# Gathered rows of the expert stages: transposed by DMA transfers instead of TensorE and ScalarE

## The reference

```python
x = x + xattn(layernorm(x), ctx)      # differential attention, 16 heads, 77 context rows per batch
# mixture of experts on h = layernorm(x), 2048 tokens, 8 experts of width 1024, two experts per token
probs = softmax(h @ gate_w.T); w, idx = top_k(probs, 2); w = w / sum(w)
for e in range(8):
    g, u = split(h @ gate_up[e].T)    # 256 -> 1024 and 1024
    acc += combine[:, e] * (silu(g) * u @ down[e].T)
x = x + acc
```

## Time and profile before

| | |
|---|---|
| median of 3 runs | 634.52 us (633.24 to 636.4) |
| profiled execution, its time | 635.76 us |
| profiled execution, span from first to last instruction | 634.0 us |
| granted TensorE clock, mean over the span | 0.905 |

### The profile page before, as it was taken

One profiled execution on the slowest core, in us unless ns is written; L12 is line 12 of the kernel. 1 busy time (PEld: TensorE's weight loads), 2 busy tenths in 40 slices (PEclk: granted clock), 3 DMA queues, 4 the chain that ended last, 5 costly groups with the idle time before them and its releaser, 6 DMA issues.

```text
span 634.0 us, 12250 instructions
## 1 busy us (share of the span) xinstructions
PE 508.0 (80%) x3882; PEld 376.9 (59%) x3897; DVE 419.5 (66%) x883; ACT 347.7 (55%) x653; POOL 253.1 (40%) x237
## 2 busy tenths in 40 slices
PE   3673798899899878601388999998999999999980
PEld 2452555666666644501266777776887777877750
DVE  6445448888888765589268888785655656646551
ACT  1210568678677577200178878775656565655530
POOL 4000634344333334100322665445555456544334
PEclk9985689898898799655799999999999999999996
DMA  4368676766756541140134776645323233332323
GB/s 160 123 167 186 183 201 173 213 161 189 210 149 179 151 151 43 42 141 0 43 89 149 173 166 158 156 105 125 60 54 56 46 66 52 59 51 44 34 24 43
DMA packets 57563, 72.55 MB, mean 114 GB/s; under 512 B 18649, under 2 KB 42841, under 8 KB 57369
## 3 DMA queue, kind: packets, MB, share of 16 engines
q1 hardware_dynamic: 45984, 56.03, 31.1%
q0 software_dynamic: 11520, 15.74, 14.9%
HBM read 49.08 MB, written 22.41 MB: 113 GB/s over the span
## 4 chain that ended last, share of the span: by engine, by line
PE 54%; DVE 17%; ACT 8%; issue 5%; DMA 4%; POOL 1%; SPq 0%; ACTq 0%; POOLq 0%; DVEq 0%
PE bank L1257 19%; PE bank L1273 10%; PE bank L1124 4%; PE bank L1110 4%; PE bank L1133 3%; PE bank L1147 3%; PE bank L1078 3%; DMA out<-FB,slot_tok 2%; DVE FB L1021 2%; DVE WE L877 2%; DVE FB L1017 2%; PE bank L1092 2%; PE bank L1228 2%; PE bank L1140 2%; PE bank L1284 1%
## 5 line engine op out<-in xcount | busy, mean ns | idle before, releaser
L1257 PE MATMUL bank<-FB,WE 128*128 128x0 bf16 x1440 | 188.5, 281 | 1.3 <-ACT FB L723 1.2
L1257 PEld LDWEIGHTS bank<-FB,WE 128*128 x1440 | 137.0, 98 | 30.7 <-issue 2.0
L1017 DVE TENSOR_TENSOR FB<-FB,bank 128x512 f32<-128x512 f32 x120 | 82.5, 687 | 105.2 <-ACT FB L730 100.4
L591 POOL DMA_INDIRECT out<-FB,slot_tok x60 | 95.7, 1595 | 103.6 <-DVE FB L1029 95.1
L730 ACT ACTIVATE FB<-bank 128x512 f32<-128x512 f32 x120 | 71.7, 598 | 102.3 <-PE bank L1257 91.3
L1273 PE MATMUL bank<-FB,WE 128*128 128x0 bf16 x720 | 104.1, 280 | 13.3 <-DVE FB L1021 10.3
L582 POOL DMA_INDIRECT FB<-x_parts,slot_tok x60 | 63.9, 1066 | 100.0 <-PE bank L1228 48.2
L1273 PEld LDWEIGHTS bank<-FB,WE 128*128 x720 | 63.8, 97 | 42.1 <-issue 27.2
L1021 DVE TENSOR_TENSOR FB<-FB 128x512 bf16<-128x512 f32 x120 | 82.4, 687 | 0.0
L525 POOL TENSOR_TENSOR WE<-FB,WE 128x1024 bf16<-128x1024 f32 x26 | 55.5, 2138 | 58.5 <-ACT WE L622 58.5
L736 ACT ACTIVATE FB<-FB 128x512 bf16<-128x512 f32 x120 | 74.9, 624 | 0.2 <-DVE FB L1017 0.2
(11 more groups left out here) (173 smaller groups left out, 660.2 us busy)
## 6 DMA issues: line engine op xcount, KB each, us to landing
FB<-w SPq DMA_DIRECT2D x26, 512.0 KB, 5.8
WE<-w SPq DMA_DIRECT2D x44, 256.0 KB
WE<-q_parts SPq DMA_DIRECT2D x32, 200.0 KB
WE<-x SPq DMA_DIRECT2D x16, 256.0 KB, 4.9
q_parts<-FB SPq DMA_DIRECT2D x32, 128.0 KB
x_parts<-WE SPq DMA_DIRECT2D x20, 128.0 KB, 4.2
out<-WE SPq DMA_DIRECT2D x20, 128.0 KB, 4.5
q_parts<-WE SPq DMA_DIRECT2D x16, 128.0 KB
```

Source lines behind the costliest of these rows:

```text
L591: pool.indirect_dma_start(out=out, out_offset=bass.IndirectOffsetOnAxis(ap=slot_tok[:, c:c + 1].bitcast(U32), axis=0), in_=y_sb[c % 2], in ...
L1017: nc.vector.tensor_tensor(hid[k % 2], hid[k % 2], up_bank[k % 2][1][:, :], ALU.mult).then_inc(h_ready, 1)
L1257: ins = nc.tensor.matmul(to, wf[:, bass.ds(at + o, P)], xgT[s % 2][:, 2 * part + kc, :].shape_from_register(long[s % 2]), start=(z == 0), ...
```

## The change

A tile is turned by four DMA transfers with `transpose=True`, from `xg[c % 2]` straight to the four blocks of `xgT[s % 2]`, issued on SP's queue. Each moves 128 rows by 128 bf16 values, 32 KB. The TensorE transposes and the ScalarE copies are gone, and with them the PSUM bank between them. Two semaphores `xg_turned`, one for each parity of the tile number, take the place of `xgt_mm` and `xgT_ready`. The late loads are now issued in one loop with the turning: four ahead, then stage 0's four tiles, then for each k the tile k % 8 of stage k // 8 + 1 (for k % 8 < 4), and behind it late load k + 4.

```diff
+            def turn_tile(s, i):
+
+                c = SUB * s + i
+                sp.wait_ge(xg_in[c % 2], 16 * (c // 2 + 1))
+                if s >= 2:
+                    sp.wait_ge(g_mm, FC * (s - 1))
+                for k in range(4):
+                    sp.dma_start(xgT[s % 2][:, k, i * P:(i + 1) * P], xg[c % 2][:, k * P:(k + 1) * P], transpose=True).then_inc(xg_turned[c % 2], 16)
+
+            def park_in():
+                sp.wait_ge(split_out, 64)
+                sp.wait_ge(late_lo, len(LATE))
+                sp.dma_start(WE[:, E - 1, 2 * W1N:EW], wd).then_inc(parked_in, 16)
+
-            for j in range(len(LATE)):
+            for j in range(LSTG):
                 load_late(j)
-            sp.wait_ge(split_out, 64)
-            sp.wait_ge(late_lo, len(LATE))
-            sp.dma_start(WE[:, E - 1, 2 * W1N:EW], wd).then_inc(parked_in, 16)
+            sp.wait_ge(idx_ready, 1)
+            for i in range(SUB):
+                turn_tile(0, i)
+            for k in range(FC * (NS - 1)):
+                if k % FC < SUB:
+                    turn_tile(k // FC + 1, k % FC)
+                if LSTG + k < len(LATE):
+                    load_late(LSTG + k)
+                if k == len(LATE):
+                    park_in()
...
             def gather(c):
                 if c >= 2:
-                    pool.wait_ge(xgt_mm, c - 1)
+                    pool.wait_ge(xg_turned[c % 2], 64 * (c // 2))
...
-            def xgT_copy(s, half):
-                act.wait_ge(xgt_mm, SUB * s + 2 * half + 2)
-                if s >= 2:
-                    act.wait_ge(g_mm, FC * (s - 1))
-                nc.scalar.activation(xgT[s % 2][:, :, 2 * half * P:2 * (half + 1) * P].rearrange("p c (i n) -> p i c n", i=2),
-                                     in_bank[:, :].bitcast(BF16).rearrange("p (i c n) -> p i c n", i=2, c=4), ACT.Copy).then_inc(xgT_ready, 1)
...
-            xgT_copy(0, 0)
-            xgT_copy(0, 1)
...
-                    if c in (3, 6) and s + 1 < NS:
-                        xgT_copy(s + 1, c // 6)
...
-            def turned_rows(s, half):
-                if 2 * s + half > 0:
-                    pe.wait_ge(xgT_ready, 2 * s + half)
-                for i in range(2):
-                    pe.wait_ge(xg_in[i], 16 * (2 * s + half + 1))
-                    A = in_bank[:, 256 * i:256 * (i + 1)].bitcast(BF16)
-                    for c in range(4):
-                        ins = nc.tensor.transpose(A[:, c * P:(c + 1) * P], xg[i][:, c * P:(c + 1) * P], ident[:, :])
-                    ins.then_inc(xgt_mm, 1)
...
                 if c == 0:
-                    pe.wait_ge(xgT_ready, 2 * s + 2)
+                    for i in range(2):
+                        pe.wait_ge(xg_turned[i], 64 * SUB // 2 * (s + 1))
...
-            turned_rows(0, 0)
-            turned_rows(0, 1)
...
-                    if c in (2, 5) and s + 1 < NS:
-                        turned_rows(s + 1, c // 5)
```

More of the change, by code:

```diff
@@ L189, in moe_attention_kernel @@
         A5, A6, A7 = bank[5], bank[6], bank[7]
-        up_bank, y_bank, in_bank, turn_bank = [bank[0:2], bank[2:4]], bank[4:6], bank[6], bank[7]
+        up_bank, y_bank, turn_bank = [bank[0:2], bank[2:4]], bank[4:6], bank[7]
         QROWS = 3 * HD + 2
@@ L268, in moe_attention_kernel @@
         rconst_ready = sem("rconst_ready")
-        xgt_mm = sem("xgt_mm")
-        xgT_ready = sem("xgT_ready")
+        xg_turned = [sem(f"xg_turned{p}") for p in range(2)]
         g_mm = sem("g_mm")
```

## The result

| | before | after |
|---|---|---|
| median of the runs | 633.88 us (633.1 to 636.4, 4 runs) | 744.35 us (743.53 to 747.58, 4 runs) |
| ratio, 95% interval | | 1.174 (1.170 to 1.179) |
| span of the profiled execution | 634.0 us | 745.8 us |
| granted TensorE clock | 0.905 | 0.839 |

The change costs 110 us, 17%. The forecast was 628.2 us with a range of 618 to 690: wrong in sign and outside the range.

A forecast was written before the change was run, and what follows sets the result against it. The prediction took TensorE to bound the kernel behind 436, and a chain over TensorE, ScalarE and VectorE before it. Removal -16.7, start +6.4 and late loads +4.0 gave -6.3 us off the median 634.5: 628.2 us, range 618 to 690.

The forecast's parts named there:

- R = 0.55: Time in us by which one transposing transfer pushes back the next on SP's queue; bounded from 0.33 to 2.1.
- turning becomes the bound: Rival: R of 1.0 to 1.5 makes the turning on SP's queue set the stages; 683 us, 665 to 720, chance 0.17.
- The signs of being wrong: SP's issues over 0.67 us, TensorE waiting at every stage, landing much over 1.8 us, or VectorE waiting for scatters.
- one transfer alone with landing: Reading of the skill page's 1309 ns that says nothing against 0.55; read as queue time it gave some 710 us.
- late loads behind turning: Stages before 436: a late load behind a tile on SP's queue is 2.2 us late, 1.4 covered; +4.0 us in five stages.
- the cost is nothing as long as that fits: Next stage's tiles are turned while a stage runs: 13.1 us against 19.4 behind 436, hidden with 6 us to spare.
- The start: Stage 0's tiles turned before the first up-projection, which moves from 316.17 to 322.6: +6.4 us.
- Behind the late weights: Stages behind 436 in the turning rival: 16R + 0.8 us for a partly uncovered landing, 20 against 19.4 at R = 1.2.
- The removal: 240 transposes and 30 copies gone: 7.4 us behind 436, 4.2 and 5.1 before it, -16.7 us in sum.
- the copies' 5.1 us are given back by the loop of ScalarE and VectorE: Rival before 436: the copies' saving is lost, sum -1.2 us; counted in the first rival's band, chance 0.15.
- Scatters: GpSimd's scatters stand behind the gather of a later stage's tile 3, which waits for a landed tile; priced at nothing.
- The stage of the 1 MB transfer: The one 1 MB transfer is issued as before, behind the last low part, and was said to cost nothing.

The follow-up runs named there:

- run 1: The changed kernel with its 240 transposing transfers made plain copies of the same number, size and waits, rows left unturned: 665.85 us, ratio 1.050 to the kernel before.
- Run 9: The changed kernel with each transposing transfer cut in two of 64 rows, 480 in place of 240: 1039.24 us in one execution.
- run 8: The changed kernel, four transfers a tile, with late loads 4 to 43 issued by ScalarE, not on SP's queue: 703.68 us, ratio 1.110 to the kernel before.
- run 2: The kernel before with the turning left out from stage 2 on, no transposes or copies there: 626.63 us, ratio 0.988.
- run 4: The changed kernel with one transposing transfer of 128 rows by 512 values a tile in place of four: 637.25 us in one execution.
- run 6: The changed kernel with one transfer a tile and the turning begun two steps earlier in SP's loop: 634.45 us, ratio 0.998 to the kernel before.
- run 7: run 6 with stage 0's four tiles turned by TensorE and ScalarE as before: 630.59 us, ratio 0.991 to the kernel before.
- run 10: run 7 with late loads 4 to 43 issued by ScalarE: 632.7 us, ratio 0.993 to the kernel before.

## Why the prediction was wrong, point by point

**R = 0.55 was the step that failed.** It measured 1.27. The sentence "because I expect issuing and not moving 32 KB to set it" was right: moving costs at most 0.18 us, issuing 1.27. But the price of an issue was taken from plain transfers, and a transposing one has its own, twice a plain one of the same block (0.60, run 1). The rival "turning becomes the bound" had R = 1.2 and a chance of 0.17. The signs of being wrong that the prediction names all showed, with one exception: the landing took 1.2 us from the end of an issue, not over 1.8. The only number that named the price was the Trainium skill's (VectorE: DVE Perf Modes, The three transpose paths), 1309 ns; the trace agrees with it at 1.27 us of queue time for 128x128. The prediction's estimate from that page was 710; the reading there as "one transfer alone with landing" was the wrong one: landing comes 2.4 us after the start of an issue.

**The rival was priced 61 us too low** (683 against 744). Some 17 of them are R again: with 1.27 in place of 1.2 its own terms (+15.3 at the start, +52, +15 and -16.7) give some 700. The other 44 are a second failure. With R = 0.64 in run 1 the prediction's sum gives 633, and 666 was measured. The step is "late loads behind turning". It took the lateness of one late load less a cover and charged it once. The trace of after shows another sum: late load and tile alternate for four steps, each as long as a tile's issues and a load, and four more steps of 2.4 us follow: 4 x 5.6 + 4 x 2.4 = 32 us, measured 28.0 to 33.5. Run 9 bears it out with longer tiles, run 8 by taking the loads off the queue. And "the cost is nothing as long as that fits" counted the turning from the stage's start; SP gets to it only past a late load that waits for a buffer. In run 1 it began at 348.2 and landed 6.13 us late.

**The start** was right in form. With R = 1.27, 309.4 + 16R + 1.8 gives 331.5, +15.3; measured +15.0. Landing was 2.4 us from the start of an issue, 1.2 from its end, where 1.8 was taken.

**Behind the late weights** 16R + 0.8 = 21.1 us were forecast for R = 1.27; the seven stages took 22.3 each. 72 issues in 100.84 us are 1.40 each:

```profile
599.76 100.84 SPq L507 DMA_TRANSPOSE FB<-FB  x72
```

Seven of them lasted 1.9 to 2.3 us instead of 1.23, which makes up 6 of the 9 us over 72 x 1.27; the rest lies in gaps between issues. What lengthens the seven stays open. The stages were also shorter before than the forecast's 20.3, 19.7 us each in these seven.

**The removal** was priced at 16.7 us, 15.5 of it in what run 2 leaves out; that run measured 7.4 (4 to 11). The 7.4 us behind 436 stood up (6.1 in seven stages, 1.1 behind them). Of the 9.3 us before it nearly none came. That the copies' 5.1 us are given back by the loop of ScalarE and VectorE was the rival, and the transposes' share there went with them. In this stretch a line's share of a chain that passes between three engines was no saving.

**Scatters** priced at nothing cost VectorE 22.3 us of waits instead of 9.9. How much of it stands on the path was not tried by itself.

**The stage of the 1 MB transfer** took 8.1 us more than before. The transfer is not the reason: it is issued behind the stage's tiles, at 520.08. With the late loads off SP's queue (run 8) the stage took 23.3 us, and 21.1 to 23.9 in the runs 4, 6, 7 and 10.

**Open:** how much of the whole is TensorE's lower clock behind the gaps wasn't tried apart from the gaps. Its matmuls' busy time grew by 22.2 us.

## What to carry to other kernels

Price a new kind of transfer by the time that it holds its issuing queue, times its count, before anything else; if no row shows the kind, the bound from below is no estimate. Then make each issue as large as it can be: here one issue of 128x512 did the work of four for the price of one, and turned a loss of 17% into no difference, and into a gain of 0.9% with the turning begun two steps earlier and the start left to TensorE.

When work is put on a queue that other work paces, ask at what time the queue reaches it and when it must be finished, not only how long it takes; and take two works that alternate on one queue as a sum for each step.

## What the runs showed of the hardware

An issue of a transposing DMA transfer from SBUF to SBUF holds SP's queue for 1.23 us (64x128 values of bf16: 1.228; 128x128: 1.232; 128x512: 1.201). A plain copy of 128x128 between the same buffers holds it for 0.60, a plain load of 256 KB from DRAM for 0.33. The transfer of 128x512 lands 3.2 us after the start of its issue (2.4 to 5.4). The DMA engine time of a 128x128 block is small: at most 2.9 us of one engine.

TensorE was at the lower level of its clock behind the long waits at the stage starts: in after, twelve matmuls take 2.18 us behind a gap of 9.28 us, with a granted clock of 0.50, and 1.19 us two steps later; in run 1 they take 2.72 us behind a gap of 6.13 us and 1.46 us two steps later in the same stage. Every such wait is therefore paid a little more than once: 22.2 us of busy time came on top of 117 us of waits at the stage starts.
